# One-hots out of digits, eight places for gathered rows, and an attention end without GpSimd, in a four-layer graph network

## The reference

```python
x = x + L0(h)   # two rounds of normalised neighbour sums (APPNP), ReLU, two products
x = x + L1(h)   # attention over the edges, 8 heads of 16
x = x + L2(h)   # neighbour means and products, twice (SAGE)
x = x + L3(h)   # three gated messages per edge, summed by destination
```

```python
q, k, v = x @ Wq + bq, x @ Wk + bk, x @ Wv + bv          # by head
e = edge_attr @ We
alpha = einsum('ehd,ehd->eh', q[dst], k[src] + e) / sqrt(16)
a = exp(alpha - segment_max(alpha, dst)[dst])
out = segment_sum(a / segment_sum(a, dst)[dst] * (v[src] + e), dst)
x_r = x @ Wskip + bskip                                    # the skip product
beta = sigmoid(concat([out, x_r, out - x_r]) @ Wbeta)
out = layernorm(beta * x_r + (1 - beta) * out) * ln_gamma + ln_beta
return x + relu(out)
```

## Time and profile before

| | |
|---|---|
| median of 3 runs | 5295.23 us |
| profiled execution, its own time | 5300.6 us |
| its span, first to last instruction | 5298.2 us |
| PE, DVE, POOL, ACT busy | 72%, 58%, 51%, 25% |
| mean granted TensorE clock | 0.817 |
| GpSimd in the attention loop | 832 gathers, 851.5 us, mean 1.023 us |
| GpSimd in the gate loop | 832 gathers, 833.3 us, mean 1.002 us |

### The profile page before, as it was taken

How to read it: one execution, slowest core, us unless ns; L and a number is a source line. 1 busy time by engine, 2 the same in 40 slices (tenths; PEclk the granted TensorE clock), 3 DMA queues, 4 the chain that set the end, 5 groups by cost and what they waited for, 6 DMA issues and landing times.

```text
span 5298.2 us, 92124 instructions
## 1 busy us (share of the span) xinstructions
PE 3810.5 (72%) x23907; PEld 2946.1 (56%) x23908; DVE 3068.8 (58%) x9503; ACT 1347.1 (25%) x3578; POOL 2681.8 (51%) x2604
## 2 busy tenths in 40 slices
PE   1000299779997677787786649999998777777784
PEld 1000166446666666676675536666666766666674
DVE  7889621131115688999998761123114667666667
ACT  0002100010002244555554240001002233333333
POOL 7777777740001776777775320000000577777776
PEclk6555599989998988999998769999999766666655
DMA  9982165446564777887786115554554333333332
GB/s 371 370 280 88 34 188 170 146 134 193 190 192 125 210 221 220 242 243 227 224 260 194 43 55 190 192 192 144 193 189 130 101 101 104 101 102 101 100 104 77
DMA packets 537346, 892.87 MB, mean 169 GB/s; under 512 B 92522, under 2 KB 392140, under 8 KB 530910
## 3 DMA queue, kind: packets, MB, share of 16 engines
q1 hardware_dynamic: 420894, 611.37, 35.9%
q0 software_dynamic: 106912, 224.30, 15.9%
q10 hardware_dynamic: 9376, 55.32, 2.8%
HBM read 732.14 MB, written 158.57 MB: 168 GB/s over the span
## 4 chain that ended last, share of the span: by engine, by line
PE 39%; POOL 32%; issue 15%; DVE 7%; DMA 4%; ACT 2%; DVEq 1%; ACTq 0%; SPq 0%; POOLq 0%
PE ps L819 23%; POOL d_adj L494 12%; POOL work L376 11%; POOL work L1289 9%; DMA d_adj<-logits,address 3%; PE ps L1010 2%; PE ps L425 2%; PE ps L1811 2%; PE ps L1417 1%; PE ps L826 1%; PE ps L1404 1%; PE ps L1406 1%; POOL hw L2041 1%; PE ps L1800 1%; DVE acc L1461 1%
## 5 line engine op out<-in xcount | busy, mean ns | idle before, releaser
L376 POOL DMA_INDIRECT work<-tab_gate,src_col x832 | 833.3, 1002 | 1296.4 <-DMA tab_gate<-logits 1024.3
L1289 POOL DMA_INDIRECT work<-tab_kv,src_col x832 | 851.5, 1023 | 881.1 <-PE ps L1010 564.9
L819 PE MATMUL ps<-hw 128*128 128x384 bf16 x5096 | 862.8, 330 | 73.7 <-DVE hw L798 34.9
L494 POOL DMA_INDIRECT d_adj<-logits,address x782 | 795.1, 1017 | 238.3 <-issue 225.8
L819 PE MATMUL ps<-hw,work 128*128 128x384 bf16 x5096 | 849.5, 327 | 20.2 <-DMA work<-d_adj 20.2
L864 DVE TENSOR_TENSOR work<-work,ps 128x128 f32 (+1 forms) x208 | 59.8, 287 | 1354.4 <-ACT work L851 1347.2
L819 PEld LDWEIGHTS ps<-hw 128*128 128x128 bf16 x5096 | 501.9, 99 | 407.0 <-DMA hw<-d_adj 51.7
L819 PEld LDWEIGHTS ps<-hw,work 128*128 128x128 bf16 x5096 | 499.6, 98 | 342.7 <-issue 20.7
L851 ACT ACTIVATE work<-ps 128x128 f32 x208 | 57.8, 278 | 1749.1 <-PE ps L819 1749.1
L1811 PE MATMUL ps<-logits,work 128*128 x1664 | 321.0, 316 | 212.3 <-ACT work L1779 165.8
L1811 PEld LDWEIGHTS ps<-logits,work 128*128 128x128 f32 x1664 | 303.8, 274 | 288.5 <-issue 288.5
(11 more groups left out here) (419 smaller groups left out, 6354.1 us busy)
## 6 DMA issues: line engine op xcount, KB each, us to landing
hw<-d_adj SPq DMA_DIRECT2D x104, 800.0 KB
work<-d_adj SPq DMA_DIRECT2D x104, 800.0 KB
d_adj<-acc SPq DMA_DIRECT2D x52, 1568.0 KB, 21.6
hw<-d_adj SPq DMA_DIRECT2D x104, 768.0 KB
work<-d_adj SPq DMA_DIRECT2D x104, 768.0 KB
work<-attr_dram SPq DMA_DIRECT2D x832, 64.0 KB
d_value<-work SPq DMA_DIRECT2D x208, 256.0 KB
hw<-d_keys ACTq DMA_DIRECT2D x49, 1024.0 KB, 8.7
```

The costliest lines, as they stand in the source:

```text
L376: pool.indirect_dma_start(rows[:, r * U + u, 0:width], None, table, bass.IndirectOffsetOnAxis(sources[:, at:at + 1], 0)).then_inc(rows_in[ ...
L494: pool.indirect_dma_start(d_adj, bass.IndirectOffsetOnAxis(address[:, tile:tile + 1], 0), counts[:, tile:tile + 1], None).then_inc(adj_out ...
L819: last = nc.tensor.matmul(at, adj_half[2 * s + hf][:, k, :], xs[:, b, :], start=b == 0, stop=b == BLOCKS - 1)
L1289: pool.indirect_dma_start(rows[:, r * U + at % U, 0:KV], None, tab_kv, bass.IndirectOffsetOnAxis(src_col[:, at:at + 1], 0)).then_inc(rows_ ...
```

## The change

Four things are changed.

1. **One-hots out of digits.** An edge's position in its block is cut into two digits of base 16. The squared distance of two positions' digits is a sum of six products, so TensorE makes a part's distances by a product with six rows (`edge_factors`, `node_factors`, bf16) and ACT makes `relu(1 - distance)` of it: the one-hot. The four rows of the edges are made once, kept in HBM (`d_factor`) and loaded part by part by SP; two more are ones. In the attention loop one product of 512 columns gives the turned one-hot, and four of 128, 39 parts later, the one for the sums (`hot_again`). VectorE makes no one-hots any more; ACT's Abs is gone.
2. **Eight places** for the parts' key and value rows; VectorE's loop is written for two turns, since a part's place depends on the turn's parity, and four turns are written out ahead of it instead of three.
3. **The end of attention without GpSimd**, and the skip product in the same pass as the queries, ahead of the attention loop; it waits in HBM (`d_h`).
4. **The last forty parts** are weighed by VectorE, their one-hots made by TensorE and ACT.

The diff, cut to its core (new positions of the rows, the products, the loops, the end and the preparation):

```diff
+        kv_places = [(rows_flat, n * KV_PART) for n in range(PARTS)] + [(w_flat, 4 * RUN + ATT_W + n * KV_PART) for n in range(2)] \
+            + [(hot_flat, n * KV_PART) for n in range(2)]
+        kv_rows = [part(buffer, at, (U, KV)) for buffer, at in kv_places]
...
-        p_q = Products(None, h, [(weight("L1_Wq"), D, take_queries)], turned=lambda g: group(t, g))
-        p_skip = Products("skip_ready", t, [(weight("L1_Wskip"), D, with_bias(t, "L1_bskip")), (w_skip_beta[:], 1, take_skip)])
+        p_q = Products(None, h, [(weight("L1_Wskip"), D, with_bias(h, "L1_bskip")), (w_skip_beta[:], 1, take_skip),
+                                 (weight("L1_Wq"), D, take_queries)], turned=lambda g: group(t, g))
...
-        UNROLLED = 3
-        STORE_BACK, LOAD_BACK, WEIGHT_BACK, WEIGH_BACK, SUM_BACK, ADD_BACK = 3, 37, 38, 39, 40, 41
+        UNROLLED = 4
+        STORE_BACK, LOAD_BACK, WEIGHT_BACK, WEIGH_BACK, HOT_BACK, SUM_BACK, ADD_BACK = 3, 37, 38, 39, 39, 40, 41
...
+            sp.dma_start(edge_factors(0, r)[0:EDGE_GIVEN, :], d_factor[:, ds(n * (U * P), U * P)]).then_inc(attr_in[r], 16)
...
+            sp.dma_start(edge_factors(1, r)[0:EDGE_GIVEN, :], d_factor[:, ds(m * (U * P), U * P)]).then_inc(value_in[r], 16)
...
-                    pool.wait_ge(sem("kv_done"), n - PARTS + 1)
+                r = n % KV_RING
+                if n >= KV_RING:
+                    pool.wait_ge(sem("kv_done"), n - KV_RING + 1)
                 for at in range(n * U, (n + 1) * U):
-                    pool.indirect_dma_start(rows[:, r * U + at % U, 0:KV], None, tab_kv,
+                    pool.indirect_dma_start(kv_rows[r][:, at % U, :], None, tab_kv,
                                             bass.IndirectOffsetOnAxis(src_col[:, at:at + 1], 0)).then_inc(rows_in[r], 16)
...
+        def hot_act(act, m, r):
+
...
+            act.wait_ge(sem("hot_turned"), m + 1)
+            nc.scalar.activation(hot_sum[:, r * U:(r + 1) * U, :], banks(1), ACT.Relu, bias=1.0, scale=-1.0).then_inc(sem("hot_by_act"), 1)
...
-                nc.scalar.activation(hot_t[:, r % RING2], banks(1), ACT.Copy).then_inc(sem("att_copied"), 1)
+                act.wait_ge(sem("att_turned"), 2 * n + 2)
+                nc.scalar.activation(hot_t[:, r % RING2], banks(1), ACT.Relu, bias=1.0, scale=-1.0).then_inc(sem("att_copied"), 1)
...
+            def turn(n, whole, r, hot_before):
+                pe.wait_ge(attr_in[r], 16 * (U + 1) * (whole + 1))
+                wait(pe, sem("att_copied"), 2 * n - 1)
+                for u in range(U):
+                    last = nc.tensor.transpose(banks(0)[:, u * D:(u + 1) * D], attr[:, r * U + u, :], ident[:])
+                last.then_inc(sem("att_turned"), 1)
                 wait(pe, sem("att_copied"), 2 * n)
+                if summed_in_loop(k, hot_before):
+                    pe.wait_ge(sem("hot_by_act"), hot_before + 1)
+                pe.sem_inc(sem("turn"), 1)
+                nc.tensor.matmul(banks(1), node_factors(0), edge_factors(0, r), start=True, stop=True).then_inc(sem("att_turned"), 1)
...
+            def hot_again(m, whole, r):
+
+                pe.wait_ge(value_in[r], 32 * (whole + 1))
+                pe.sem_inc(sem("turn"), 1)
+                pe.wait_ge(sem("att_copied"), 2 * (m + HOT_BACK + 1))
+                pe.sem_inc(sem("turn"), 1)
                 for u in range(U):
-                    nc.tensor.transpose(banks(0)[:, u * D:(u + 1) * D], attr[:, r * U + u, :], ident[:])
-                for u in range(U):
-                    last = nc.tensor.transpose(banks(1)[:, u * P:(u + 1) * P], hot[:, r * U + u, :], ident[:])
-                last.then_inc(sem("att_turned"), 1)
...
+            def weigh(m):
+                k = stretch_of(m)
+                dve.wait_ge(sem("exp_ready"), FIRST_PIECE[k + 1])
+                tail_values_arrived(dve, m)
+                at = tail_message(m)[:, :, 0:D].rearrange("p u (h d) -> p u h d", h=HEADS)
+                wide = part_weights(k, (m - FIRST_PART[k]) // PARTS, m % PARTS).unsqueeze(3).broadcast_to((P, U, HEADS, HEAD_DIM))
+                nc.vector.tensor_tensor(at, at, wide, ALU.mult).then_inc(sem("msg_weighed"), 1)
...
+            for n in range(GROUPS + 2):
+                if n < GROUPS:
+                    normalise(n)
+                if 0 <= n - 1 < GROUPS:
+                    weigh_out(n - 1)
+                if 0 <= n - 2:
+                    sum_out(n - 2)
+            dve.wait_ge(sem("beta_out"), GROUPS)
+            nc.vector.tensor_tensor(stat[:, 0, :], stat[:, 0, :], stat[:, 6, :], ALU.add).then_inc(sem("beta_dve"), 1)
             dve.wait_ge(sem("h_moved"), 32)
...
+            for g in range(GROUPS):
+                nc.vector.tensor_tensor(group(t, g), group(t, g), group(w, g), ALU.subtract).then_inc(sem("mix_out"), 1)
...
+            for n in range(GROUPS + 1):
+                if n < GROUPS:
+                    scale_rows(n)
+                if n:
+                    stats_of(n - 1)
+                if n < GROUPS:
+                    shift_rows(n)
+                    onto_x(n)
...
+        def gate_sp(sp):
+            def load(i, r):
+                n = i * PARTS + r
+                wait(sp, sem("gate_turned"), n - PARTS + 1)
+                sp.dma_start(edge_factors(0, r)[0:EDGE_GIVEN, :], d_factor[:, ds(n * (U * P), U * P)]).then_inc(attr_in[r], 16)
+            edge_loop(sp, [(0, load)])
...
-                nc.scalar.activation(hot_t[:, r % RING2], banks(0), ACT.Copy).then_inc(sem("gate_copied"), 1)
+                nc.scalar.activation(hot_t[:, r % RING2], banks(0), ACT.Relu, bias=1.0, scale=-1.0).then_inc(sem("gate_copied"), 1)
+                if not isinstance(i, int) or i:
+                    act.wait_ge(sem("win_done"), gate_sums.done0 + U * ((i - 1) * PARTS + r + 1))
+                nc.scalar.activation(hot[:, r * U:(r + 1) * U, :], banks(1), ACT.Relu, bias=1.0, scale=-1.0).then_inc(sem("gate_copied"), 1)
...
+                nc.tensor.matmul(banks(0), node_factors(0), edge_factors(0, r), start=True, stop=True)
                 for u in range(U):
-                    last = nc.tensor.transpose(banks(0)[:, u * P:(u + 1) * P], hot[:, r * U + u, :], ident[:])
+                    last = nc.tensor.matmul(banks(1)[:, u * P:(u + 1) * P], edge_factors(0, r)[:, u * P:(u + 1) * P], node_factors(0),
+                                            start=True, stop=True)
                 last.then_inc(sem("gate_turned"), 1)
...
+            sp.wait_ge(sem("factors_made"), 1)
+            for k in range(EDGE_GIVEN):
+                sp.dma_start(d_factor[k, :].rearrange("(c p e) -> p c e", p=P, e=P), edge_factor[k]).then_inc(sem("factors_out"), 16)
+            sp.wait_ge(sem("factors_made"), 2)
+            for at in EDGE_FACTORS:
+                sp.dma_start(node_rows_bf[at:at + FACTORS, :], node_factor[0:1, :, :]).then_inc(sem("factors_out"), 16)
...
+            chain.after(nc.vector.tensor_scalar(edge_f[LAST], edge_f[REL], -1.0, float(P), ALU.max, ALU.min))
+            chain.after(nc.vector.tensor_copy(edge_digit_i[0], edge_f[LAST]))
+            chain.after(nc.vector.tensor_scalar(edge_digit_i[1], edge_digit_i[0], DIGIT.bit_length() - 1, None, ALU.arith_shift_right))
+            chain.after(nc.vector.tensor_copy(edge_digit[0], edge_digit_i[1]))
+            chain.after(nc.vector.scalar_tensor_tensor(edge_digit[1], edge_digit[0], -float(DIGIT), edge_f[LAST], ALU.mult, ALU.add))
+            for k in range(2):
+                nc.vector.tensor_tensor(edge_factor[2 * k], edge_digit[k], edge_digit[k], ALU.mult)
+                last = nc.vector.tensor_copy(edge_factor[2 * k + 1], edge_digit[k])
+            last.then_inc(sem("factors_made"), 1)
+            nc.vector.memset(factor_rows[EDGE_FACTORS[0]:P, :], 1.0)
...
+            dve.wait_ge(sem("factors_out"), 16 * (EDGE_GIVEN + len(EDGE_FACTORS)))
...
-            p_q.dve(dve)
-            for g in range(GROUPS):
-                nc.vector.tensor_tensor(group(x, g), group(x, g), group(h, g), ALU.add).then_inc(sem("x_added"), 1)
+
+            def residual(g):
+                for k in ((0, 1) if g == 0 else (g + 1,)):
+                    if k < GROUPS:
+                        nc.vector.tensor_tensor(group(x, k), group(x, k), group(h, k), ALU.add).then_inc(sem("x_added"), 1)
+                dve.wait_ge(sem("x_added"), g + 1)
+            p_q.dve(dve, residual)
```

More of the change, by code:

```diff
@@ L336, in sem @@
             return sems[name]
[L338 removed]
+        rows_in = [sem(f"rows_in{r}") for r in range(KV_RING)]
         attr_in = [sem(f"attr_in{r}") for r in range(PARTS)]
@@ L1167, in stretch_loop, with stretch_loop_of_two @@
                         step(i, r)
+        def stretch_loop_of_two(engine, k, step):
+            turns = STRETCH_PARTS[k] // PARTS
+            first = UNROLLED if turns > UNROLLED + 1 else turns
+            for p in range(first * PARTS):
+                step(p // PARTS, p % PARTS)
+            if first < turns:
```

(5 more changed lines are left out.)

280 lines of the change are left out of this document (138 added, 142 removed).

## The result

The changed kernel takes 5420.51 us (median of 4 runs, 5416.35 to 5425.97), the kernel before beside it 5295.88 (5293.65 to 5301.56): a ratio of 1.0234, with a 95% interval of 1.0218 to 1.0249. The forecast was 5232 within 5160 to 5290, and 0.88 for faster. It was wrong in sign. The nearest case was rival 2, with a chance of 0.09 and a time of 5371.

A forecast was written before the change was run, and what follows sets the result against it. No engine bounds it throughout: VectorE and TensorE in turn pace attention, GpSimd's gathers the gate loop, TensorE close. 4 + 0 - 26 + 6 - 25 - 22 = -63 from 5300.6 gives 5237.6, less 5.4 is 5232 us; range 5160 to 5290.

The forecast's parts named there:

- rival 2: Gate loop becomes TensorE's at a granted clock of 0.5, attention loop's TensorE slips too: total 5371, chance 0.09.
- Gate loop, -22: Gate loop: without VectorE's 208 one-hots gathers stretch less, some 5.15 us a part instead of 5.25 to 5.30: -22 us.
- it would carry a part in (1020 - 46.6)/195 = 4.99 us: Gate loop: TensorE's time per part at the mean granted clock of 0.63, set beside GpSimd's 5.03.
- Attention loop, -26: Attention loop without 208 VectorE one-hots: -14 us over four and a half stretches, -12 in the first 40 parts.
- the turning round: Attention loop: 1.63 us from VectorE's last sum add through TensorE's passes to the next key row; a part 4.85 for 4.95.
- First 40 parts, -12: Attention loop's first 40 parts, without sums: GpSimd alone sets the pace, 0.3 us a part saved, -12 us.
- Tail, +6: Last forty parts: VectorE gains the weighing and loses the one-hot, 2.35 us a part, 94 us against 88: +6.
- End, -25: End of attention without GpSimd and the skip product's evictions: 101.8 us for 126.6, so -24.8 us.
- Preparation, +4: Before the first dense pass: about 12 us of new VectorE work beside the scatter, a third of it counted: +4 us.
- Rival 3: Attention and gate loops stay, TensorE's round hiding the one-hot; only the end and first parts gain: total 5275, chance 0.22.
- Rival 1: Attention loop becomes GpSimd's, as the turning round shrinks and eight places bridge the maxima: -80, total 5178, chance 0.17.
- Rival 4: Preparation costs all its 12 us twice, at scatter and first multiplication, else as forecast: total 5252, chance 0.10.

The follow-up runs named there:

- a_load_g_order: Changed kernel with TensorE's gate-loop one-hot products ahead of the sums, and ACT instead of SyncE issuing the attention loop's factor loads: 5206.45 us, ratio 0.9833 to the kernel before.
- a_load_g_old_order3: a_load_g_order with the gate loop's one-hots made by VectorE as before, TensorE's altered order kept: 5257.31 us, ratio 0.9924 to the kernel before.
- g_fill2: Changed kernel with four needless fp32 products ahead of each part's logits in the gate loop: 5551.35 us, ratio 1.0482 to the kernel before.
- g_old2: Changed kernel with the gate loop's one-hots as in the kernel before: 5302.70 us, ratio 1.0017 to the kernel before.
- g_order: Changed kernel with TensorE's gate-loop one-hot products ahead of the sums of three parts before: ratio 0.9982 on a slower chip; 5259.38 us repeated on the first kind.

## Why the prediction was wrong

- **Gate loop, -22: +118.** The gain that was forecast is real, and the next bound was wrong. The stretching went as forecast (a mean of 0.946 us), and is worth 55 us against the old one-hots in the new order. The step that failed is "it would carry a part in (1020 - 46.6)/195 = 4.99 us". It took TensorE's capacity from a loop whose mean clock was 0.63 and carried that clock over; the changed loop was granted 0.50 throughout and took 5.90 us a part. At the low clock has the round, 5.62 us, above GpSimd's 5.0; this was the safe figure, and it belonged in the sum and not in a rival. Why the clock stays down is open, as said above; that it did, and what a round then takes, is shown. The wait for ACT's copy, 1.11 us, was taken as given; with the sums put into it the kernel is 161 us faster.
- **Rival 2, 5371 at 0.09.** Its price of 1169 us for the loop was worked out for a round of 5.62; it became 5.90. (1169 for 1105 is +64, not the +70 that the prediction puts into its sum.) Its mark, a mean clock under 0.55, came true. What spoke against it, that the clock rises "again and again", ended with the edit, so 0.09 was too low. Its second part, a slip of TensorE in the attention loop (+21), came in size (+20) by another cause, SyncE's queue; that is luck.
- **Attention loop, -26: +20.** What failed is a step left out: of the two added DMAs a part I counted none on SyncE's queue, which the earlier trace rows do not show. The room was 4.95 - 4.25 = 0.7 us a part, for 1.15 of new issues: the 0.45 that is over, for 168 parts with sums, is 76 us at most (an estimate), and the swap of the queue gave 53 back.
- **The same loop with the loads off SyncE's queue: -26.4.** That this is the -26 of the forecast is luck. Between the 17th and the 31st part of a stretch the key rows are 5.01 us apart in a_load_g_order and 5.02 in the kernel before (means of four stretches), where 4.85 was forecast; the shortest rounds are 4.63 for 4.64. So the turning round did not shrink: from part 40 on the key row waits for TensorE's sums 139.5 us, for 29.9 before, and this wait fills the place of the one-hot. The loop still gains 20.4 us over these parts, and over the same parts the key row's waits for gathered rows fall from 16.7 us to none. With four places the gain is 11.2 and these waits are 8.9. So most of the gain goes with rows that come in time. The eight places, of which the prediction said "by itself brings nothing where VectorE is behind", give 9.2 us of it; no run parts the rest. The 168 parts are also 5.25 stretches, and not the four and a half of the sum. GpSimd's waits at the maxima did not fall under 2 us for 13.06: the longest is 22.6 us in the changed kernel and 11.8 in a_load_g_order.
- **First 40 parts, -12: -6** in a_load_g_order (1922.0 for 1928.0); the first key row's 14 us later start (1733.1 for 1719.2), put at nothing, was not wholly made up.
- **Tail, +6: +6.5**, at 2.27 us a part for 2.35. **End, -25: -29.** The size of each step held; the last part took 31.7 us (3076.2 to 3107.9) for 33.5.
- **Preparation, +4: +2.** Of some 8 us of VectorE work beside scatters 1.7 were lost. The rule of the Trainium skill, page "SBUF — State Buffer", section "Who interferes with whom", would have made it 12, by the prediction's estimate; here two-operand instructions (618.93, 620.05) lengthened the scatter beside them by 0.52 us, no more, so the trace does not bear out a whole exclusion for them. The scatter at 639.7 does, with 6.66 us beside one VectorE addition of 6.69 (638.82).
- **Rival 3** (nothing from a hidden one-hot) falls for the gate loop with a_load_g_old_order3; for the attention loop's rounds, 5.01 us for 5.02, it was right. **Rival 1** (GpSimd's attention loop) falls with the 140.3 us for TensorE's sums. **Rival 4** did not come.

## What to carry to other kernels

Where an edit takes work off the engine that bounds a loop, name the next bound at the lowest clock that the loop has shown, not at its mean. Count each added DMA on the queue that issues it, with a timeline of that queue before, as if it were an engine. And where an engine waits in every round for a copy of what it has just made, put work of an earlier round between the two before taking work away elsewhere.

## What the runs showed of the hardware

TensorE, busy for 950 of 950 us, was granted 1.2 GHz throughout (g_fill2), while at 76% busy in the same stretch the mean was 0.64 (g_old2, 722.6 of 950 us), and at 71% busy it was 0.50 again (g_order, 846.3 of 1200 us). Nothing that I added (products, transposes, six-row products) moved it either way. And a small DMA takes its issuing queue nearly as long as a large one: 0.30 us for the 4 KB of a factor load (2567.12), 0.36 for the 256 KB of a value store (2567.69).
